# A mixture-of-experts layer behind a gated recurrence: layer 0's feed-forward computed inside the recurrence, in half-precision parts

## The reference, cut to what matters

```python
def step(h, xs):                                   # 512 steps, h0 = 0
    z = sigmoid(xzt + h @ U_z + vz)
    r = sigmoid(xrt + h @ U_r + vr)
    hh = tanh(xht + r * h @ U + vh)
    h_new = (1.0 - z) * h + z * hh
...
# _L0_ffn_ref, with x the states of the recurrence
weights = einsum('bsd,do->bso', x, w_r) + b_r
threshold = top_k(weights, s // 2)[0][:, -1]
hidden = gelu(x @ W1 + b1, approximate=False)      # 256 -> 1024
blk = hidden @ W2 + b2                             # 1024 -> 256
out = where(weights > threshold, blk, x)
```

## Time and profile before

| what | value |
|---|---|
| median of 3 runs | 2202.97 us (2202.05 to 2204.38) |
| the profiled execution: its own time | 2206.26 us |
| its span in the profile | 2204.3 us |
| TensorE busy, matmuls | 2130.6 us, 97% |
| TensorE busy, weight loads | 1950.1 us, 88% |
| VectorE busy | 1540.5 us, 70% |
| ScalarE busy | 854.4 us, 39% |
| recurrence, first to last L472 | 23.0 to 1046.4 us |
| `dense`, first L710 to its last | 1051.6 to 1402.7 us |

### The profile page before, as it was taken

The page is one execution under the profiler, slowest core; times in us unless marked ns, Lnnn a source line. Parts: engine busy times, 40 slices in busy tenths (PEclk is TensorE's granted clock), DMA queues, the critical chain, the costliest instruction groups (busy, mean ns, idle before and its releaser), DMA issues. The chain is left out here.

```text
span 2204.3 us, 80152 instructions
## 1 busy us (share of the span) xinstructions
PE 2130.6 (97%) x31922; PEld 1950.1 (88%) x31929; DVE 1540.5 (70%) x8765; ACT 854.4 (39%) x3350; POOL 432.1 (20%) x592
## 2 busy tenths in 40 slices
PE   8999999999999999998999999999999999999997
PEld 7898888888888889887778888866999999999997
DVE  6777777777777777777454455495577777777775
ACT  3333444433333333333555676633222222222221
POOL 0000000000000000000000000154455555555553
PEclk9999999999999999999999999999999999999999
DMA  5000000000000000000002123210888888888882
GB/s 161 4 4 4 4 4 4 4 4 4 4 4 4 4 4 4 4 4 4 1 1 85 62 92 110 108 59 27 302 269 278 270 278 273 274 274 274 274 272 62
DMA packets 55543, 213.54 MB, mean 97 GB/s; under 512 B 11578, under 2 KB 40960, under 8 KB 46976
## 3 DMA queue, kind: packets, MB, share of 16 engines
q1 hardware_dynamic: 36276, 184.41, 22.7%
q0 software_dynamic: 17408, 23.61, 5.7%
q10 hardware_dynamic: 1484, 0.40, 0.1%
HBM read 192.82 MB, written 15.57 MB: 95 GB/s over the span
## 5 line engine op out<-in xcount | busy, mean ns | idle before, releaser
L1405 PE MATMUL bank<-xe,ring 128*128 128x160 f32 x3072 | 438.4, 299 | 0.7 <-DVE xe L1455 0.7
L1405 PEld LDWEIGHTS bank<-xe,ring 128*128 128x128 f32 x3072 | 422.6, 190 | 0.9 <-issue 0.9
L1448 DVE STREAM_TRANSPOSE turned<-ye 32x64 f32<-32x64 f32 x1240 | 291.2, 235 | 16.2
L568 PE MATMUL bank<-keep_part,Us 128*128 128x4 f16 x6132 | 285.8, 168 | 0.4 <-DVE keep_part L482 0.3
L568 PEld LDWEIGHTS bank<-keep_part,Us 128*128 128x128 f16 x6132 | 242.9, 105 | 12.3 <-DVE keep_part L482 0.4
L568 PE MATMUL bank<-h_part,Us 128*128 128x4 f16 x6144 | 242.3, 167 | 0.8 <-DVE h_part L502 0.8
L1360 POOL DMA_INDIRECT out_rows<-res,to_row x128 | 192.3, 1503 | 242.8 <-DVE res L1467 204.7
L1433 ACT ACTIVATE gate_f<-bank 128x160 f32<-128x160 f32 x384 | 116.4, 303 | 287.9 <-PE bank L1405 280.3
L568 PE MATMUL bank<-step_high,Us 128*128 128x4 f16 x4096 | 192.3, 169 | 34.1 <-DVE step_high L486 2.8
L340 ACT ACTIVATE r_h<-bank 128x8 f32<-128x8 f32 x512 | 92.7, 181 | 338.6 <-PE bank L568 338.6
L1414 PE MATMUL bank<-mid,ring 128*128 128x160 f32 x1536 | 221.0, 300 | 2.1 <-DVE mid L1476 2.1
(11 more groups left out here) (234 smaller groups left out, 3563.7 us busy)
## 6 DMA issues: line engine op xcount, KB each, us to landing
ring<-in_ew SPq DMA_DIRECT2D x64, 2304.0 KB
raw<-in_L_cond_ew SPq DMA_DIRECT2D x16, 1024.0 KB, 6.7
ctx_rows<-rows SPq DMA_DIRECT2D x2, 1280.0 KB, 7.0
dense_w<-in_L_ffn_W SPq DMA_DIRECT2D x2, 1024.0 KB, 6.6
raw<-in_L_cond_sw SPq DMA_DIRECT2D x2, 1024.0 KB, 8.2
out_rows<-orow SPq DMA_DIRECT2D x4, 512.0 KB, 2.9
out_rows<-res,to_row POOLq DMA_INDIRECT x128
xT<-in_xT SPq DMA_DIRECT2D x2, 864.0 KB, 9.1
```

What stands on the lines that cost most here:

```text
L568: last = nc.tensor.matmul(pre[g][q][:, jj, m, :], Us[:, g, p, k, m * P:(m + 1) * P], x[part][:, k * B:(k + 1) * B], start=False, stop=Fals ...
L1405: last = nc.tensor.matmul(bank[f % UPS][:, s_ * CAP:(s_ + 1) * CAP], w1[u][:, k, s_ * FFN + f * P:s_ * FFN + (f + 1) * P], xe[e % 2][:, k] ...
L1448: last = nc.vector.transpose(y[:, :, q, :], ye[e % 2][q * SQ:(q + 1) * SQ, :, j * SQ:(j + 1) * SQ])
```

## The change

Layer 0's feed-forward no longer has its own four units. The 12 full spans are fed through it inside the recurrence, one span behind (window w computes span w - 1), with the state and hidden parts and both weight matrices in fp16 parts scaled by powers of two found on the chip. Each window adds 48 up and 48 down matmuls of 160 columns to TensorE's queue, placed by step; ScalarE adds 8 Gelus, 2 output copies and 2 clears, VectorE 16 splits. The hidden tiles use the free columns of banks 6 and 7, the outputs those of banks 0 to 3. The last 32 steps (128 columns) and the ranking follow in `dense`: those of batch 0 before the shared expert, the ranking of batches 1 to 3 between the shared expert's tiles, and the gate of the experts moves into unit 2 of the shared expert. The gates are tanh of half the argument, with the halves and ones folded into VectorE's operations; z takes one more ScalarE operation. ScalarE preloads Gelu's table in place of Sigmoid's.

```diff
+SPAN = 40
+LAST = S // SPAN * SPAN
...
-                nc.scalar.preload_act_table(ACT.Sigmoid)
+                nc.scalar.preload_act_table(ACT.Gelu)
...
-                    nc.scalar.activation(r, pre_of(0, q, jj), ACT.Sigmoid, scale=inv[0]).then_inc(s_r, 1)
+                    nc.scalar.activation(r, pre_of(0, q, jj), ACT.Tanh, scale=inv[0]).then_inc(s_r, 1)
                     act.wait_ge(s_zp, j + 1)
-                    nc.scalar.activation(nz[:], pre_of(1, q, jj), ACT.Sigmoid, scale=inv[3]).then_inc(s_nz, 1)
-                    nc.scalar.activation(z, pre_of(1, q, jj), ACT.Sigmoid, scale=inv[1]).then_inc(s_z, 1)
+                    nc.scalar.activation(nz_one, pre_of(1, q, jj), ACT.Tanh, scale=inv[3]).then_inc(s_nz, 1)
+                    nc.scalar.activation(tz[:], pre_of(1, q, jj), ACT.Tanh, scale=inv[1]).then_inc(s_tz, 1)
+                    act.wait_ge(s_tz, j + 1)
+                    nc.scalar.activation(z, tz[:], ACT.Identity, scale=2.0 ** (STATE_EXP - 1), bias=lift[:, 0:1]).then_inc(s_z, 1)
...
+        FFN_HIGH_AT = ((0, 27), (0, 28), (0, 33), (0, 34), (0, 39), (1, 0), (1, 1), (1, 2))
+        FFN_LOW_AT = [(0, at) for at in range(28, 40)] + [(1, at) for at in (0, 0, 1, 1, 2, 2, 3, 3, 4, 5, 6, 9, 14, 15, 20, 21, 26, 27, 32, 33)]
+        GELU_AT = (9, 10, 15, 16, 21, 22, 27, 28)
+        SPLIT_AT = ((10, 11), (12, 13), (16, 17), (18, 19), (22, 23), (24, 25), (28, 29), (30, 31))
+        BLOCK_AT, CLEAR_AT, CLEAR_FINAL_AT = (1, 2), (33, 34), 5
+        def up_products(window, jj):
+            if window == FINAL:
+                if jj < 6:
+                    return 4 * jj, 4 * jj + 2, 4 * jj + 4
+                return (2 * jj + 12, 2 * jj + 14, 2 * jj + 14) if jj < 18 else (0, 0, 0)
+            at = jj // TERMS * 2 * TERMS + jj % TERMS * 3
+            return (at, at + 1, at + 3) if jj < 4 * TERMS and jj % TERMS < 4 else (0, 0, 0)
+        def down_products(window, jj):
+            if window == FINAL:
+                return (2 * jj - 12, 2 * jj - 10) if 6 <= jj < 30 else (0, 0)
+            if jj in (16, 17):
+                return 2 * jj - 32, 2 * jj - 30
+            if 22 <= jj < 32:
+                return 2 * jj - 40, 2 * jj - 38
+            return (3 * jj - 72, 3 * jj - 69) if jj >= 32 else (0, 0)
...
                             ahead[jj]()
+                        first, middle, end = up_products(span, jj)
+                        if span:
+                            for n in range(first, middle):
+                                ffn_up(span, n)
                         pe.wait_ge(s_rhhi, m)
                         recur(2, q, jj, reset, 0)
...
                             recur(0, nq, njj, kept, 0)
+                        if span:
+                            for n in range(middle, end):
+                                ffn_up(span, n)
+                            if down_products(span, jj)[1]:
+                                pe.wait_ge(s_z, m)
+                            for n in range(*down_products(span, jj)):
+                                ffn_down(span, n)
+                        if m < S:
                             pe.wait_ge(s_klo, m)
                             recur(0, nq, njj, kept, 1)
...
-                    nc.vector.tensor_tensor(h_part[:, 0], step_in[:], keep[:], ALU.add).then_inc(s_hhi, 1)
+                    nc.vector.scalar_tensor_tensor(out=h16_of(0, j), in0=step_in[:], scalar=2.0, in1=keep[:],
+                                                   op0=ALU.mult, op1=ALU.add).then_inc(s_hhi, 1)
-                    nc.vector.tensor_tensor(h_new, step_in[:], keep[:], ALU.add).then_inc(s_h, 1)
+                    nc.vector.scalar_tensor_tensor(out=h_new, in0=keep[:], scalar=0.5, in1=step_in[:],
+                                                   op0=ALU.mult, op1=ALU.add).then_inc(s_h, 1)
...
-                    nc.vector.tensor_tensor(h_part[:, 1], h_new, h_part[:, 0], ALU.subtract).then_inc(s_hlo, 1)
+                    nc.vector.scalar_tensor_tensor(out=h16_of(1, j), in0=h_new, scalar=2.0, in1=h16_of(0, j),
+                                                   op0=ALU.mult, op1=ALU.subtract).then_inc(s_hlo, 1)
...
+                def scale_step(bits, jj):
+                    if 3 <= jj < 7:
+                        peak_of(up_loaded, 0, jj - 3)
+                    if jj in (11, 12, 14, 15):
+                        peak_of(down_loaded, 1, (11, 12, 14, 15).index(jj))
...
+                scores(0)                      # dense, TensorE
+                for f in range(4):
+                    tail_up_tile(f)
+                turn_scores(0)
+                tail_up_tile(4)
+                count(0)
+                for f in range(KH):
+                    tail_down(f)
+                    if f + 5 < KH:
+                        tail_up_tile(f + 5)
...
                 for b in range(B):
+                    pe.wait_ge(s_xlo, (b + 1) * KD)
                     for f in range(KH):
+                        up_tile(b, f, w1[0], [v[:, :, b] for v in xs])
+                        if b == 0 and f == 0:
+                            scores(1)
+                        if b == 0 and f == 1:
+                            turn_scores(1)
+                        if b == 0 and f == 5:
+                            count(1)
+                        if b == 1 and f == 1:
+                            count(2)
+                        if b == 1 and f == 4:
+                            scores(3)
+                        if b == 1 and f == 6:
+                            turn_scores(3)
+                    down_half(b, 0, w2[0])
+                    if b == 0:
+                        scores(2)
+                    if b == 1:
+                        count(3)
+                    if b == 2:
+                        gate()
+                    down_half(b, 1, w2[0])
+                    if b == 0:
+                        turn_scores(2)
...
+                scored(0)                      # dense, ScalarE; VectorE has tail_low(f) for each f, compare(0) after the third
+                for f in range(KH):
+                    tail_hidden(f)
+                    if f:
+                        tail_high(f - 1)
+                tail_high(KH - 1)
+                nc.scalar.preload_act_table(ACT.Gelu_apprx_tanh)
...
+                        hidden(b, f, b1[:, 0])
+                        if b == 0 and f == 1:
+                            scored(1)
+                        if b == 1 and f == 5:
+                            scored(3)
```

More of the change, by code:

```diff
@@ L511, in _ @@
-                    if i is not None and 1 <= n <= LOWS:
-                        dve.wait_ge(s_nhi, i + 1)
-                        whole, high, low = next_piece(i, (n - 1) * LOW, n * LOW)
-                        nc.vector.tensor_tensor(low, whole, high.bitcast(F32), ALU.subtract).then_inc(s_nlo, 1)
+                        low_inputs(span + 2, (lows.index(jj),))
+                    ffn_vector(span, jj)
             @block.tensor
@@ L556, in _ @@
                 nc.tensor.matmul(bank[1][:, GATES * C2:GATES * C2 + GATES * KD], bias_rows[:], ident[0:GATES * KD, 0:GATES * KD],
-                                 start=True, stop=True, skip_group_check=True).then_inc(s_bt, 1)
-                state = [h_part[:, p] for p in range(2)]
+                                 start=True, stop=True, skip_group_check=True).then_inc(s_v, 1)
                 kept = [keep_part[:, p] for p in range(2)]
@@ L595, in _ @@
                         recur(0, q, jj, step, 1).then_inc(s_rp, 1)
+                        state = [h16_of(p, STARTS[span] + jj - 1) for p in range(2)]
                         pe.wait_ge(s_hhi, m)
@@ L704, in _, with scores, turn_scores @@
             def _(pe):
-                def up_tile(m, f, up, w, x):
-                    if f >= len(up):
+                def scores(b):
+                    if b:
+                        pe.wait_ge(s_m, b)
+                    for k in range(KD):
+                        last = nc.tensor.matmul(bank[0][:], wr_rep[:, k], hist[:, k, b], start=(k == 0), stop=(k == KD - 1))
+                    last.then_inc(s_sp, 1)
+                def turn_scores(b):
+                    pe.wait_ge(s_s, b + 1)
+                    for j in range(S // P):
+                        last = nc.tensor.transpose(bank[1][:, j * P:(j + 1) * P], ws[:, j * P:(j + 1) * P], ident[:])
+                    last.then_inc(s_tp, 1)
@@ new lines, in count, with tail_up_tile @@
+                def count(b):
+                    pe.wait_ge(s_ge, b + 1)
+                    for j in range(S // P):
+                        last = nc.tensor.matmul(bank[0][:], ones_bf[:], ge[:, j], start=(j == 0), stop=(j == S // P - 1))
+                    last.then_inc(s_cnt, 1)
+                def tail_up_tile(f):
+                    if f >= 4:
+                        pe.wait_ge(s_tf, before + f - 3)
+                    for i in range(KD * len(MEET)):
+                        k, (w, x) = i // len(MEET), MEET[i % len(MEET)]
```

(11 more changed lines are left out.)

691 lines of the change are left out of this document (468 added, 223 removed).

## The result

The changed kernel takes 2195.69 us (median of 7 runs, 2194.54 to 2196.91); the kernel before takes 2203.32 us beside it (7 runs). The ratio is 0.9963 (95% interval 0.9952 to 0.9975), faster by 0.4%; the medians lie 7.6 us apart, where 20.8 were forecast. The sign holds, most of the parts do too, and the size is 13 us short. One run of experiment 1 (2464.1 us) and one of before beside experiments 1 to 4 (4176.0) were slow ones, and their ratios leave them out.

A forecast was written before the change was run, and what follows sets the result against it. The prediction held that one serial loop through TensorE, ScalarE and VectorE sets the 2.0 us recurrence step, while TensorE is truly busy in `dense`. 2204.3 + 46.9 - 67.7 = 2183.5 us, on the median 2182; 8-in-10 range 2136 to 2210.

The forecast's parts named there:

- (c): Recurrence steps with an input product: scalar_tensor_tensor makes the low state part 0.03 us late, no slack, +11.5 us.
- (e): `dense` up to the first chosen expert: 123.0 us instead of 190.75, 19.5 of it before the first shared tile; -67.7 us.
- (b): Added matmuls before `step_high`: two fit in 0.30 us, three in steps 32 to 39 run 0.10 over, +8.8 us.
- (a): Before `rh_high`: one up matmul behind the input product has no cover in 16 steps of 11 windows, +23.4 us.
- Gap 1: TensorE's wait before `rh_high` in a recurrence step: 0.23 us, gone in steps with an input product.
- Gap 2: TensorE's wait before `step_high` in a recurrence step: 0.29 to 0.31 us, only 0.14 of it showing as idle.
- (d): VectorE's and ScalarE's additions beside the steps: peak reductions +2.4 and weight pieces +0.8, splits at nothing; +3.2 us.
- The clock did not rise: First rival: the clock rises in the recurrence, 160 columns cost 0.066 us, added matmuls fit; 2138 us, chance 0.17.
- not 0.14: Second rival: the wait before `step_high` covers only the 0.14 us that shows as idle, +53; 2235 us, chance 0.12.
- Gelu and tanh did not alternate tables: Third rival: no shared table, so ScalarE loads one before and after each of 96 Gelus; 2438 us, chance 0.03.
- the fourth rival: `dense` gives back only 47: chosen experts' weights come late or VectorE's rankings delay shared tiles; 2203 us, chance 0.06.

The follow-up runs named there:

- experiment 1: Changed kernel with the up matmul between input product and `rh_high` moved before the low `keep_part`, beside the other two: 2172.86 us, ratio 0.9867 to the kernel before.
- experiment 2: Changed kernel with the low state part made by a plain subtraction, its doubling left out: 2193.44 us, ratio 0.9964 to the kernel before.
- Experiment 3: Changed kernel with the low state part written to a contiguous tile, the feed-forward in the recurrence reading zeros instead: 2184.61 us, ratio 0.9920 to the kernel before.
- experiment 4: Changed kernel with the states copied into the history by ScalarE instead of GpSimd, one step later: 2189.53 us, ratio 0.9946 to the kernel before.
- experiment 5: Changed kernel without the feed-forward inside the recurrence (zeros for the first 480 steps), tanh gates kept: 2162.51 us, ratio 0.9819 to the kernel before.
- experiment 7: Changed kernel with 16-bit states laid out step by step, so state writes are contiguous and up matmuls read strided: 2242.00 us, ratio 1.0183 to the kernel before.
- experiment 10: Changed kernel with the edits of experiments 1, 4 and 6, plus low state written contiguously and copied by ScalarE for the feed-forward: 2158.03 us, ratio 0.9801.
- Experiment 6: Changed kernel with batch 0's count after the fourth `tail_down` and two score copies one hidden tile earlier: 2187.78 us, ratio 0.9935 to the kernel before.

## Why the prediction was right in sign and wrong in size

Of the 13.2 us that are missing, 5.4 lie in the recurrence, 3.6 in `dense` up to the first chosen expert, 1.3 behind it, and 2.9 in the yardstick: before's profiled execution is that much above its median, after's is its median, so the difference of the spans (10.5) is not that of the medians (7.6). I had carried the forecast over unchanged. The largest term that failed is (c), 8.3 us too low; (e) is 3.6 too low, and that (b) was 4.6 too high hid half of the error of (c) by luck.

- **(a) Gap 1, +23.4: right.** Up steps stand 2.175 - 2.044 = 0.131 above their neighbours, 176 of them: 23.1. Experiment 1 takes it away.
- **(b) Gap 2, +8.8: too high by 4.6.** Three downs cost 0.048 in steps 36 to 39 and 0.047 in 32 to 35, 88 steps: 4.2. The cover is 0.40 - 0.05 = 0.35, not 0.30, and in a product step three cost nothing on top of (c), as experiment 1 shows. The two are not added: a step takes the longer of what (c) leaves it and some 2.034. With (c) whole, steps 32 to 35 take 2.047 without any downs (experiment 5) and 2.040 to 2.047 with three; with (c) halved or gone they take 2.033 to 2.034 with three (experiments 3, 7 and 10). So the 2.1 us of steps 32 to 35 could as well stand under (c).
- **(c) Late low state part, +11.5: the step that failed.** The place was right: no slack behind eight of twelve matmuls, only in product steps. The price was not 0.03 but 0.051 in 388 steps, 19.8 us. The term was sized from the distance of two scalar_tensor_tensor; experiment 2 shows that the kind of operation costs nothing. What costs is where both parts are written: every element in another place 80 bytes on, L730 0.167 for 0.141 and L741 0.195 for 0.167, 0.054 together; over all steps L741 starts 0.271 behind L730's start where L502 started 0.251 behind L494's, and ends 0.467 behind it for 0.419. Experiment 3 takes one of the two back (0.025), experiment 7 both (0.05). In rows 4 both outputs were contiguous; the diff's new layout was there to be read, and I costed the instruction's name and not its operand.
- **(d) Beside the steps, +3.2: too low by 1.9.** The excess over the medians rose from 5.5 to 10.6 us. I costed the splits at nothing with 10 us if the cover failed. The cover fails in the steps in which GpSimd copies, 2.8 of the 5.1 (4.1 for 1.3), and experiment 4 takes 2.4 back; of the other 2.3, span 0 holds 1.7 (its peak reductions stand in eight steps that exceed their median by 0.2 to 0.3 each), span 1 0.4 and the last window 0.6, and the rest gives 0.4 back. So what I had priced at 3.2 took 2.1, and the splits under GpSimd's copies, priced at nothing, 2.8.
- **Recurrence:** 23.1 + 4.2 + 19.8 + 5.1 = 52.2 of the measured 52.3.
- **(e) `dense`, 123.0: 126.7.** The shared units are right (103.8 for 103.5). The tail is 3.4 late: a tile takes 1.22 (1108.21 to 1109.44 is 1.23) instead of 1.1, since ScalarE waits for VectorE each time, and the chain of tiles stands still while TensorE's count waits for the ranking. I counted the ranking as beside; in TensorE's queue it is ahead. Experiment 6 recovers 2.7 of the tail and 3.5 behind it.

**The rivals.** The clock did not rise: 0.50 in the records of experiment 1, the lower level, and an up matmul holds TensorE for 0.13, not 0.066. Gap 2 covers more than the forecast, not 0.14. Gelu and tanh did not alternate tables: ScalarE's loads up to the routed part are one at the start, and then in `dense`:

```profile
L388 ACT ACT_TABLE_LOAD x1 | 1.3, 1283 | 4.6 <-issue 4.6
L1149 ACT ACT_TABLE_LOAD x1 | 1.3, 1283 | 0.0
```

With 96 Gelus of 483 ns between them and tanh in every step, one load served both. The Trainium skill's page ScalarE: Activation LUTs (section "Table sets: the hidden batching unit") names no tanh in Gelu's set; here the measurement decides. From the first to the last up matmul of the chosen experts it is 163.1 us before and after, and the shared units take 103.8 for 103.5, so the fourth rival did not happen either.

## What to carry to other kernels

Price a moved write by its access pattern as well as by its operation: the same 8 elements cost 26 to 28 ns more when they are written 80 bytes apart, and two such writes on a serial chain cost 0.05 us a step, 388 times. Two costs that end in the same wait are not added: the larger one counts. Before choosing a gap for added work, compare gaps by what waits at their end; here a shift of one matmul from one gap to the other was worth 21 us in the recurrence, nearly three times the whole change. A matmul that waits for another engine's side task blocks everything behind it in its queue, so queue it where its operand is already there.

## What the runs showed of the hardware that I had not expected

- A strided moving operand at the lower clock: 160 columns of fp16 16 bytes apart hold TensorE for 0.31 us, 0.15 when contiguous.
- A VectorE operation on 8 elements a partition: 0.195 us written 80 bytes apart, 0.167 contiguous.
- A GpSimd multiply of 0.53 us stretches a VectorE operation with two inputs from 0.378 to 0.65, and it ends 0.18 to 0.19 behind the multiply.
- The granted clock stays at 0.50 for 1061 us of experiment 1, from 24.8 us on, with TensorE's records at 98% of the time.
